# Cross-attention scores as one float32 matmul a head, in place of three passes over rounded halves of K and Q

## What is computed

```python
a = layer_norm(audio_kv, ln_gamma, ln_beta)          # over 512, eps 1e-5
Q = (hidden_states @ Wq.T)   # (32, 112, 16 heads, 32)
K = (a @ Wk.T)               # (32, 375, 16 heads, 32)
V = (a @ Wv.T)
scores = einsum('bhtd,bhsd->bhts', Q, K) * 32 ** -0.5
scores = where(mask, scores, -inf)
attn = softmax(scores, axis=-1)
out = einsum('bhts,bhsd->bhtd', attn, V).reshape(B, Tt, D) @ Wo.T
return hidden_states + tanh(gate) * out
```

## Time and profile before

| | us |
|---|---|
| device time, three runs | 1136.5, 1140.73, 1141.64 |
| median | 1140.73 |
| span of the profiled execution | 1134.9 |
| its own device time | not shown apart from the span |
| PE busy in it | 1100.3 (97%) |
| PE weight loads busy | 921.6 (81%) |
| DVE busy | 861.4 (76%) |
| ACT busy | 679.0 (60%) |
| POOL busy | 565.0 (50%) |
| mean granted clock of PE | 0.987 of full speed |

### The profile page before, as it was taken

One profiled execution on the slowest core, in us unless ns is written; L12 is line 12 of the kernel. 1 busy time (PEld: TensorE's weight loads), 2 busy tenths in 40 slices (PEclk: granted clock), 3 DMA queues, 4 the chain that ended last, 5 costly groups with the idle time before them and its releaser, 6 DMA issues.

```text
span 1134.9 us, 28841 instructions
## 1 busy us (share of the span) xinstructions
PE 1100.3 (97%) x9614; PEld 921.6 (81%) x9614; DVE 861.4 (76%) x2438; ACT 679.0 (60%) x1811; POOL 565.0 (50%) x745
## 2 busy tenths in 40 slices
PE   9799899999999999999999999999999999999997
PEld 8798788878888888888888888888888887888885
DVE  4643888887877788888787788888787778887764
ACT  2414565656666666666666666666666666666653
POOL 1344746555555566655455566655554566655100
PEclk9899899999999999999999999999999999999997
DMA  9453223222333233323333333323333333331000
GB/s 270 168 152 70 69 73 72 55 76 74 83 85 85 72 85 73 66 64 75 77 85 85 80 77 77 70 56 75 77 85 85 82 75 76 67 67 45 10 17 17
DMA packets 53010, 89.55 MB, mean 79 GB/s; under 512 B 15184, under 2 KB 35664, under 8 KB 52976
## 3 DMA queue, kind: packets, MB, share of 16 engines
q1 hardware_dynamic: 52400, 88.19, 31.8%
q10 hardware_dynamic: 576, 0.92, 0.3%
HBM read 81.66 MB, written 7.44 MB: 79 GB/s over the span
## 4 chain that ended last, share of the span: by engine, by line
PE 72%; DVE 16%; DMA 5%; issue 4%; POOL 1%; ACT 1%; SPq 1%; DVEq 0%; POOLq 0%
PE bank L690 43%; PE bank L747 14%; PE bank L847 6%; DVE shared_f L668 6%; PE bank L770 6%; DVE stats L574 4%; DVE shared_f L649 3%; PE bank L712 2%; DMA qT<-in_wkT 2%; DMA row_stats<-row_stat 1%; DMA rows<-in_ctx 1%; DVE mv L577 1%; POOL cn L404 1%; ACT shared_f L513 1%; DMA stat_bc<-row_stats 0%
## 5 line engine op out<-in xcount | busy, mean ns | idle before, releaser
L404 POOL TENSOR_TENSOR cn<-cn,stat_bc 128x375 f32<-128x375 f32 x256 | 258.8, 1043 | 387.4 <-DMA stat_bc<-row_stats 371.1
L513 ACT ACTIVATE shared_f<-shared_f,ntop 112x375 f32<-112x375 f32 x512 | 306.3, 601 | 14.3 <-DVE ntop L649 14.1
L690 PE MATMUL bank<-shared_r,w_k 128*128 128x376 f32 x1536 | 295.9, 342 | 0.0
L690 PE MATMUL bank<-w_v,shared_r 128*125 128x512 f32 x1152 | 291.7, 402 | 0.1
L649 DVE CUSTOM_DVE_ANT_0 shared_f<-bank,mask_b 112x375 f32<-112x375 f32 x512 | 258.6, 543 | 32.1 <-PE bank L770 30.8
L690 PEld LDWEIGHTS bank<-shared_r,w_k 128*128 128x128 f32 x1536 | 260.4, 190 | 0.3
L747 PEld LDWEIGHTS bank<-ident,shared_f 112*125 112x125 f32 x1536 | 199.1, 190 | 67.9 <-issue 27.9
L690 PEld LDWEIGHTS bank<-w_v,shared_r 128*125 128x125 f32 x1152 | 206.7, 186 | 46.1 <-issue 0.5
L668 DVE TENSOR_SCALAR shared_f<-shared_f,rden 112x375 f32<-112x375 f32 x512 | 240.3, 531 | 4.5
L747 PE MATMUL bank<-ident,shared_f 112*125 112x112 f32 x1536 | 222.1, 281 | 20.2 <-DVE shared_f L668 19.6
L536 ACT ACTIVATE shared_f<-bank 125x448 f32<-125x448 f32 x256 | 139.0, 543 | 166.8 <-PE bank L747 166.8
(11 more groups left out here) (49 smaller groups left out, 816.4 us busy)
## 6 DMA issues: line engine op xcount, KB each, us to landing
rows<-in_ctx SPq DMA_DIRECT2D x32, 750.0 KB
cn<-in_ctxT SPq DMA_DIRECT2D x32, 750.0 KB, 12.2
stat_bc<-row_stats SPq DMA_DIRECT2D x32, 375.0 KB, 4.4
xy<-in_x SPq DMA_DIRECT2D x32, 224.0 KB, 2.5
out<-xy SPq DMA_DIRECT2D x32, 224.0 KB, 2.3
shared_f<-in_xT SPq DMA_DIRECT2D x7, 896.0 KB, 8.9
mask_u<-in_mask SPq DMA_DIRECT2D x32, 41.0 KB, 3.1
qT<-in_wqT SPq DMA_DIRECT2D x4, 256.0 KB, 5.5
```

The lines of the kernel that those rows point to most:

```text
L404: last = pool.tensor_tensor(chunk, chunk, stat_bc[:, w, :], op)
L513: last = act.activation(prob[0:T, r % 2, h, :], prob[0:T, r % 2, h, :], ACT.Exp, bias=ntop[0:T, r % 2, h:h + 1], scale=-1.0, accum_out=den ...
L690: last = pe.matmul(dst, l, m, start=(start and k == 0), stop=(stop and k == len(pairs) - 1))
```

## The change

K's projection and Q stay unsplit: `kT` and `qs` become float32 tiles, laid over the place where the two halves stood, with the layout of what follows kept. ACT copies K out of its bank as float32 and signals `k_done` itself; DVE's subtraction (L678) and the semaphore `k_hi` go. POOL copies Q as float32 and signals `qr_done`; its subtraction (L360), and the wait between the two, go. PE issues four float32 matmuls a slot, one a head, each opening and closing its bank's sum, where there were twelve float32r matmuls in three rounds over the heads. The waits ahead of the scores stay.

```diff
@@ -86,9 +86,13 @@
         at, xr = cut_r(0, 2, 2, KT, GN)
         at, wq = cut_r(at, 2, KT, D)
         at, cT = cut_r(0, 2, 2, KT, SE)
-        at, kT = cut_r(at, 2, 2, SE)
-        at, qr = cut_r(at, 2, 2, KT, T)
+
+        scores_at = nc.sbuf_base - 4 * (2 * WN + 4 * KT * GN) + 4 * at
+        at, _ = cut_r(at, 2, 2, SE)
+        at, _ = cut_r(at, 2, 2, KT, T)
         at, oT = cut_r(at, 2, 2, KT, T)
+        kT = nc.alloc_sbuf_tensor_at("kT", [128, 2, SE], F32, offset=scores_at)
+        qs = nc.alloc_sbuf_tensor_at("qs", [128, 2, KT, T], F32, offset=scores_at + 4 * 4 * SE)
 
 
         shared_f = sb("shared_f", [128, 2 * ST * D + 2 * HC * S + HC * ST * T])
@@ -157,14 +161,12 @@
         row_stat_done = sem("row_stat_done")
         ln_part = sem("ln_part")
         ln_done = sem("ln_done")
-        qr_step = sem("qr_step")
         qr_done = sem("qr_done")
         mask_step = sem("mask_step")
         mask_done = sem("mask_done")
         c_hi = sem("c_hi")
         c_done = sem("c_done")
         k_mm = sem("k_mm")
-        k_hi = sem("k_hi")
         k_done = sem("k_done")
         v_mm = sem("v_mm")
         v_done = sem("v_done")
@@ -355,10 +357,7 @@
                 src = qT[:, bass.ds(i * 2 + c, 1), :, :].rearrange("p a c t -> p (a c) t")
                 if not first_two(i, c):
                     wait_apart(pool, s_mm, i * LOOP + (c - 1) * KT)
-                pool.tensor_copy(qr[:, c % 2, 0, :, :], src).then_inc(qr_step, 1)
-                wait_apart(pool, qr_step, i * 2 + (c + 1))
-                pool.tensor_tensor(qr[:, c % 2, 1, :, :], src, qr[:, c % 2, 0, :, :].bitcast(F32),
-                                   ALU.subtract).then_inc(qr_done, 1)
+                pool.tensor_copy(qs[:, c % 2, :, :], src).then_inc(qr_done, 1)
 
             def convert_mask(i, c):
                 m = mask_b[0:T, c % 2, :]
@@ -526,7 +525,7 @@
 
                 if live(i, LOOP, r + 2, SLOTS):
                     act.wait_ge(k_mm, i * LOOP + (r + 3))
-                    act.activation(kT[:, r % 2, 0, :], bank[KB][:, 0:SE], ACT.Copy).then_inc(k_hi, 1)
+                    act.activation(kT[:, r % 2, :], bank[KB][:, 0:SE], ACT.Copy).then_inc(k_done, 1)
 
             def transposed(i, r, g):
                 if live(i, LOOP, r - 1, SLOTS):
@@ -673,12 +672,6 @@
                 if not early(i, r):
                     context_lo(i, r)
 
-                if live(i, LOOP, r + 2, SLOTS):
-                    dve.wait_ge(k_hi, i * LOOP + (r + 3))
-                    dve.tensor_tensor(kT[:, r % 2, 1, :], bank[KB][:, 0:SE],
-                                      kT[:, r % 2, 0, :].bitcast(F32), ALU.subtract) \
-                        .then_inc(k_done, 1)
-
             slots(dve, slot)
 
 
@@ -764,11 +757,10 @@
                     pe.wait_ge(k_done, i * LOOP + (r + 1))
                     if not isinstance(i, int) or LOOP * i + r > 0:
                         pe.wait_ge(max_done, i * (LOOP * HC) + r * HC)
-                    for k, (a, d) in enumerate(PASSES):
-                        for h in range(HC):
-                            rows = slice(HD * h, HD * h + HD)
-                            last = pe.matmul(bank[h][0:T, 0:SE], qr[rows, c, a, u, :], kT[rows, q, d, :],
-                                             start=(k == 0), stop=(k == len(PASSES) - 1))
+                    for h in range(HC):
+                        rows = slice(HD * h, HD * h + HD)
+                        last = pe.matmul(bank[h][0:T, 0:SE], qs[rows, c, u, :], kT[rows, q, :],
+                                         start=True, stop=True)
                     last.then_inc(s_mm, 1)
 
                 if before:
```

## The result

Over 18 runs each, the kernel after takes 1143.23 us (median; 1137.68 to 1145.69) and the one before 1138.87 us (1134.85 to 1142.14). The ratio is **1.0036, 95% interval 1.0021 to 1.0051**: 0.36% slower, 4.4 us. That is inside the range of the prediction and within 0.5% of no change, but the forecast had a gain of 4.7 us: the sign is wrong. The time lies in the range only because the range took in the rivals too; the forecast's own range, 1131 to 1141 us, misses it.

The account below looks back on a forecast made before the run. PE was taken to bound most slots, a ring through DVE, POOL and SP the 27 late periods. Late periods -5.4 us, the 20 other slots +0.8, an allowance of 0.1, rounded to -4.7, gave 1136.0 us; range 1121 to 1151.

Parts of the forecast that it names:

- The ring: Loop from output product through store, loads, statistics, POOL's adds, DVE's scaling and transposes back to it: 31.87 us, forecast 31.67.
- late slot: Second slot of each batch, where PE's transposes wait for DVE's last probability scaling; said to cost 0.79 us each.
- DVE's residual: DVE's subtraction L678 delays the output product in late slots; removing it gives back 0.20 us in each of 27.
- POOL's split: POOL's Q subtraction goes; the statistics store comes 1.3 us sooner but still queues behind `cn`, so no gain.
- POOL's start comes sooner: Rival: the statistics store sets the return, so POOL's adds begin 1.3 us sooner and late waits go; 1124 us, chance 0.08.
- Halves side by side on row strips: Score matmuls on PE: four heads run side by side, as two sets of 0.32 us each, like PV's matmuls.
- strict order: Rival: score halves queue head by head on PE, +1.0 us a slot, 1248 us, chance 0.12.
- no overlap: Rival: no score matmuls run side by side on PE's row strips, +1.97 us a slot, 1371 us, chance 0.05.
- so 0.81 us in all, +0.04 us a slot: Scores on PE: four float32 matmuls last 0.81 us where twelve float32r ones took 0.77, so +0.04 us a slot.
- The scores are not in it: Claim that PE's score matmuls are no part of the loop that sets the late period of 31.87 us.
- in the 27 late periods the longer scores are absorbed: PE's own period, 31.24 us, stays under 31.67, so longer scores cost nothing there; 27 x -0.20 = -5.4 us.
- the collision shifts the wrong way: Rival: DVE's scaling misses its gap between POOL's adds in half of 27 periods, 0.95 us each; 1149 us, chance 0.09.

Follow-up runs that it names:

- The second profiles: The changed kernel and the kernel before, each run once more unchanged for a second profiled execution: 1143.37 and 1138.68 us.

## Why the prediction failed, step by step

- **The ring** (output product, transfers, adds, scaling, output product): right. Its first part is the same in all these variants, and cutting it at the scaling took the late slot's delay away (a period of 31.21 us, 31.08 expected).
- **DVE's residual, 0.20 us in each of 27 late slots:** right. 0.21 to 0.22 us in the ring's last part, 5.9 us in sum, shown from both sides (taken from before, put back into after). The forecast's own gain, 5.4 us, was there; the scores took it back and more.
- **POOL's split, nothing:** right. The store's step grew to 8.4 us in the period shown (8.5 forecast; 8.9 on average), and putting the subtraction back moved nothing. The rival that POOL's start comes sooner is false.
- **Halves side by side on row strips:** right. The rivals of strict order and of no overlap are false. In strict order of the records, head by head, two sets would take over 1.7 us; they take 0.90. The Trainium skill, TensorE: Matmul & The Clock Gate, section Packing small matmuls, has matmuls strictly ordered in start and end. The trace doesn't say which head a record belongs to; if a head's two records stand next to each other in the program, as the rival had it, the measurement says otherwise for float32 matmuls on four row strips. If the order holds for whole matmuls alone, there is no conflict.
- **Failed: "so 0.81 us in all, +0.04 us a slot".** The term was mis-sized: +0.13 us. I priced the first set like one that follows a set of its own kind, and it costs 0.09 us more. The trace of the kernel before had the number: the first set of its scores ends after 0.43 us and a later record lasts 0.33. With it the sum would have been 0.90 us. In the 20 slots outside the late periods this makes 2.6 us, not 0.8.
- **Failed: "The scores are not in it", and so "in the 27 late periods the longer scores are absorbed".** They pass no time through PE, but they set when DVE's scaling starts. In the mean period the scaling starts 6.09 us after the slot's first score, not 5.94; and since POOL's start hangs on the last result and not on PE's slots, and the slot starts later behind that result (18.05 us, not 17.82), POOL starts earlier against it. The two together move POOL's lead by some 0.35 us towards a missed gap; I had put it at "some 0.1 us". Seven to eleven of 26 periods then pay some 1.1 us more behind the fourth add, and the ring's middle part grows by 0.33 to 0.39 us, which more than eats the 0.22.
- **The chance of "the collision shifts the wrong way", 0.09:** far too low. It is what happened, at about half its price (7 to 11 of 26 periods, not half). My evidence against it, that the first and the last late slot wait alike, said nothing on it: what mattered was how near the periods already stood to the edge, and the nearest of the kernel before leads by 1.63 us, 0.07 us from it. POOL's lead, read off for all 27 late slots, would have shown that.

The sum as it stands now, for the span: ring (32.01 - 31.87) x 27 = +3.8 us; 20 other slots x 0.12 to 0.13 = +2.5 us; the rest of the 2.8 us between the two spans, -3.5 us, lies ahead of and behind these periods. The second profiles (31.93 and 32.09 us, spans of 1136.9 and 1141.5) leave -2.2 us there. Part of it may be what the first slots gain without L678; no run settles it. The lead drifts from period to period with the ring's first part and with nothing else: that part varies by 0.39 us (standard deviation, kernel after), the slot's start behind the result by 0.03 and the scaling's behind the slot's start by less than 0.01. So what makes some gaps missed lies between the result and POOL's start, on the way through the loads and the statistics; where in it, I have not settled.

## What to carry to other kernels

Work that shortens one engine can lose where two engines take turns on a resource: look not only at how long the critical chain is, but at when its steps fall against the other engine's blocks, and how near the nearest one stands to the next block. A cheap wait that orders the two (POOL behind DVE's scaling) was worth 2.0% here; taking DVE's 128 subtractions out was worth 0.7%. And price an operation by its first instance in a row as well as by the ones that follow their own kind.

## What the runs showed of the hardware

- A scaling on DVE that meets POOL's adds takes 0.395 us at its shortest and up to 1.162 (view below). In the missed gap shown above three scalings end 0.21 us behind the end of an add each, by the single records (behind the third, the fourth and the fifth): they get through between the adds.

```profile
L667 DVE TENSOR_SCALAR shared_f<-shared_f,rden x512: 395/411/1162, 112.7 to 1125.5; 112x375 f32<-112x375 f32 x171
```

  With the wait in place four scalings take 1.39 us. The Trainium skill, SBUF — State Buffer, section Who interferes with whom, calls it an exclusive lock on the port pair that the two engines share, held for a whole instruction; that fits these numbers. For a DVE operation with one input the section asks for a two-port mode, and no run here shows the mode. The missed gap is what it does when POOL's adds follow each other: the loss comes in whole adds.
- Float32 matmuls of 32 rows, four heads on four row strips, show two records each, and a set of four records of 376 columns takes 0.32 us; a slot's four are whole in 0.90 us, where twelve float32r ones made the scores in 0.77. The three rounded passes that the change removes were the faster way on PE, at 128 subtractions on DVE.
- The first of several sets of four score matmuls costs 0.09 us more than the next ones, with float32r operands and with float32 ones.
- A store of 2.9 KB behind 1.5 MB of loads on the same queue returned after 7.2 or 8.4 us according to when it was issued, in both cases so that the load went out 13.1 us behind that of `cn`. In the last period the step took 2.5 us: there the load of `rows` is missing, and that of `cn` was issued 6.5 us before the store.

```profile
1018.18 0.43 SPq L257 DMA_DIRECT2D cn<-in_ctxT  x1
```
